# Five stages of a two-layer kernel written out sequence by sequence instead of in loops of two, with small moves in the first attention

## The reference, cut to what matters

```
x = layernorm(x + gated_state_space(x))       # layer 0, "attn": norm, 64-channel projection, norm,
                                              #   long convolution (kernel of 512 taps), gate, output
x = layernorm(x + latent_attention_and_moe(x))# layer 0, "ffn": rms norm, low-rank q/k/v with rotary parts,
                                              #   16 causal heads of 8; then a shared expert and 7 routed
                                              #   experts (top 2) of width 128
x = layernorm(x + attention(x))               # layer 1, "attn": 16 causal heads of 8, dense
x = layernorm(x + moe(x))                     # layer 1, "ffn": top 2 of 8 experts of width 512
```

## Time and profile before

| | us |
|---|---|
| median of 3 runs (lowest, highest) | 3305.35 (3304.07, 3309.35) |
| the profiled execution's own time | 3310.25 |
| its span, first to last instruction | 3308.5 |

### The profile page before, as it was taken

The page is one execution under the profiler, slowest core; times in us unless marked ns, Lnnn a source line. Parts: engine busy times, 40 slices in busy tenths (PEclk is TensorE's granted clock), DMA queues, the critical chain, the costliest instruction groups (busy, mean ns, idle before and its releaser), DMA issues. The chain is left out here.

```text
span 3308.5 us, 51694 instructions
## 1 busy us (share of the span) xinstructions
PE 2513.5 (76%) x15431; PEld 1777.0 (54%) x15431; DVE 2159.5 (65%) x8218; ACT 1411.2 (43%) x2540; POOL 1300.9 (39%) x2522
## 2 busy tenths in 40 slices
PE   1455873999999999488887599999999732688972
PEld 1323662656665656366666465666666431576751
DVE  5733764777777777388887477767777340467674
ACT  0001321665555566112121266666666411576851
POOL 3210012555455554223221255555555457222166
PEclk9997995999999999699999599999999755799986
DMA  2143002232232231211110222222212251476762
GB/s 30 30 143 115 22 10 37 34 47 41 29 46 39 31 46 28 90 48 48 61 34 4 41 38 33 32 40 40 34 26 40 64 204 58 148 226 214 252 187 72
DMA packets 198712, 228.44 MB, mean 69 GB/s; under 512 B 48621, under 2 KB 148814, under 8 KB 190478
## 3 DMA queue, kind: packets, MB, share of 16 engines
q1 hardware_dynamic: 188302, 207.69, 26.1%
q0 software_dynamic: 8192, 16.79, 1.6%
q10 hardware_dynamic: 2048, 2.10, 0.2%
HBM read 132.55 MB, written 58.10 MB: 58 GB/s over the span
## 5 line engine op out<-in xcount | busy, mean ns | idle before, releaser
L1422 PE MATMUL banks<-Kb,Qb 96*128 96x512 f32 (+3 forms) x2048 | 625.5, 353 | 75.8 <-issue 37.0
L1431 PE MATMUL banks<-Qb,Kb 98*128 98x512 f32 (+1 forms) x1408 | 580.0, 418 | 27.3 <-ACT mha_prob L1323 16.5
L1095 DVE CUSTOM_DVE_ANT_0 mha_junk<-banks,mha_mask 128x512 bf16<-128x512 f32 (+3 forms) x1024 | 455.5, 488 | 212.8 <-PE banks L1422 200.2
L1095 DVE CUSTOM_DVE_ANT_0 mla_junk<-banks,mla_mask 128x512 bf16<-128x512 f32 (+3 forms) x1024 | 455.3, 488 | 190.0 <-PE banks L1422 156.9
L1422 PEld LDWEIGHTS banks<-Kb,Qb 96*128 96x128 f32 x2048 | 377.1, 199 | 327.1 <-DVE mha_nm L1095 105.8
L1323 ACT ACTIVATE mla_prob<-banks 128x512 f32<-128x512 f32 (+1 forms) x704 | 372.9, 559 | 304.0 <-PE banks L1431 302.7
L1323 ACT ACTIVATE mha_prob<-banks 128x512 f32<-128x512 f32 (+1 forms) x704 | 373.5, 559 | 269.8 <-PE banks L1431 265.7
L1218 POOL TENSOR_SCALAR_AFFINE_SELECT mla_prob<-mla_prob 128x128 f32<-128x128 f32 (+2 forms) x704 | 237.8, 346 | 330.6 <-PEq L1430 323.4
L1218 POOL TENSOR_SCALAR_AFFINE_SELECT mha_prob<-mha_prob 128x128 f32<-128x128 f32 (+2 forms) x704 | 238.1, 347 | 301.0 <-PEq L1430 289.7
L1431 PEld LDWEIGHTS banks<-Qb,Kb 98*128 98x128 f32 x1408 | 273.3, 195 | 115.5 <-issue 97.9
L2198 DVE TENSOR_TENSOR moe_hl<-moe_h,moe_hh 128x512 fp32r<-128x512 f32 x212 | 146.1, 690 | 199.6 <-issue 95.1
(11 more groups left out here) (436 smaller groups left out, 5181.1 us busy)
## 6 DMA issues: line engine op xcount, KB each, us to landing
moe_wt<-expert_rows SPq DMA_DIRECT2D x53, 1024.0 KB
conv_tz<-conv_kernel SPq DMA_DIRECT2D x16, 1024.0 KB, 6.2
moe_xg<-slots SPq DMA_DIRECT2D x53, 256.0 KB
results<-moe_yt SPq DMA_DIRECT2D x53, 256.0 KB
Kb<-mla_kh SPq DMA_DIRECT2D x32, 256.0 KB, 5.5
Qb<-mla_qh SPq DMA_DIRECT2D x128, 64.0 KB
Kb<-mha_kh SPq DMA_DIRECT2D x32, 256.0 KB, 5.5
Qb<-mha_qh SPq DMA_DIRECT2D x128, 64.0 KB
```

Of the source, the lines that this page charges most:

```text
L1095: last = dve.tensor_tensor_reduce(junk[:, k % 3, at:at + w], ps[:, bank1(k), at:at + w], mask[:, L - w:L], -1.0, BIG, ALU.add, ALU.min, nm ...
L1422: last = pe.matmul(ps[:, bank1(k), at:at + w], Qb[0:MROW, u, g, h, j * P:(j + 1) * P], Kb[0:MROW, u, g, 0:w], start=True, stop=True)
L1431: pe.matmul(ps[:, bank2(g, k), 0:WIDE[k]].rearrange("p (x w) -> p x w", x=heads), Kb[0:MROW + 2, u, grp, kb * P:(kb + 1) * P], Qb[0:MROW + ...
```

## The change: what it does

In the walks of five stages (input, gate, both attentions, shared and routed experts) the loop over pairs becomes straight code, one copy for each sequence; `settle` goes from all of them, and semaphores count up through the stage. In the input stage the loops of ScalarE and TensorE go too. The loops of SyncE in the input, gate and experts stages, of GpSimd in the gate stage and all of the convolution stage stay. In the attentions' tables some places are moved: in the latent one the two key products, the statistics, `inverse_rms` and the two `prepare` steps; in both of them `NEXT`, by one unit.

```diff
@@ walk_sequences
     body(0, 0, False, True, True)
-    c.settle()
-    with eng.Fori(0, (NB - 2) // 2, 1) as i:
-        for v in range(2):
-            body(i * 2 + (v + 1), (v + 1) % 2, True, True, True)
-        c.settle()
+    for n in range(1, NB - 1):
+        body(n, n % 2, True, True, True)
     body(NB - 1, (NB - 1) % 2, True, True, False)
@@ input_stage, ScalarE (TensorE in the same way, its body unchanged)
-                with act.Fori(0, NB // 2, 1) as i:
-                    for u in range(2):
-                        act.wait_ge(t_ready, c.next(t_ready))
-                        act.activation(xth[:, u, :], ps[:, 1 + u, :], ACT.Copy).then_inc(th_ready, 1)
-                    c.settle()
+                for n in range(NB):
+                    u = n % 2
+                    act.wait_ge(t_ready, c.next(t_ready))
+                    act.activation(xth[:, u, :], ps[:, 1 + u, :], ACT.Copy).then_inc(th_ready, 1)
@@ attention_stage, tables
         if latent:
-            KEYS = dict(pe=((0, 10), (0, 11)), turn=(1, 1), add=(1, 2), act=(1, 5), low=(1, 7))
+            KEYS = dict(pe=((0, 11), (1, 0)), turn=(1, 1), add=(1, 2), act=(1, 5), low=(1, 7))
             QUERIES = dict(pe=((1, 6), (1, 8)), turn=(1, 10), add=(1, 11), act=(2, 3), low=(2, 5))
-            NEXT_XS = dict(stats=(2, 8), rms=(2, 11), scale=((3, 1), (3, 3)))
+            NEXT_XS = dict(stats=(2, 6), rms=(2, 9), scale=((3, 0), (3, 2)))
...
-        NEXT = dict(pe=(3, 6), act=(3, 7), dve=(3, 9))
+        NEXT = dict(pe=(3, 7), act=(3, 8), dve=(3, 10))
@@ attention_stage, walk
             body(0, 0, "first", True, True, False)
-            c.settle()
             body(1, 1, "inner", True, True, False)
-            c.settle()
-            with eng.Fori(0, (NB - 4) // 2, 1) as i:
-                for v in range(2):
-                    body(i * 2 + (v + 2), v, "inner", True, True, True)
-                c.settle()
+            for n in range(2, NB - 2):
+                body(n, n % 2, "inner", True, True, True)
@@ swiglu_experts_stage, walk
             tile(0, 0, True, 2)
-            c.settle()
-            with eng.Fori(0, (NB - 4) // 2, 1) as i:
-                for v in range(2):
-                    tile(i * 2 + (v + 1), (v + 1) % 2, False, 2)
-                c.settle()
-            for n in range(NB - 3, NB):
+            for n in range(1, NB):
                 tile(n, n % 2, False, min(2, NB - 1 - n))
```

More of the change, by code:

```diff
@@ L429, in _ @@
                 pe.sem_inc(d_free, 2)
[L430 to L444, removed]
-                    c.settle()
+                for n in range(NB):
+                    u = n % 2
+                    pe.wait_ge(xh_ready, c.next(xh_ready))
+                    for b in range(BLK):
+                        last = pe.transpose(ps[:, 1 + u, b * P:(b + 1) * P], xh[:, u, b, :], flip[:, :])
+                    last.then_inc(t_ready, 1)
+                    pe.wait_ge(t_split, c.next(t_split))
+                    pe.wait_ge(d_free, c.next(d_free))
+                    for b in range(BLK):
+                        o = ps[:, 3 + u, b * NC:(b + 1) * NC]
+                        tok = slice(b * P, (b + 1) * P)
+                        pe.matmul(o, xth[:, u, tok], wdh[:, :], start=True, stop=False)
+                        pe.matmul(o, xth[:, u, tok], wdl[:, :], start=False, stop=False)
+                        last = pe.matmul(o, xtl[:, u, tok], wdh[:, :], start=False, stop=True)
+                    last.then_inc(d_ready, 1)
 def convolution_stage(nc, io, ps, U, kd, yd):
```

## The result

| | us |
|---|---|
| kernel before, same chip and session, median of 4 | 3307.35 (3304.07 to 3312.17) |
| changed kernel, median of 4 (lowest, highest) | 3219.80 (3218.61, 3221.26) |
| ratio, 95% interval | 0.9734 [0.9717, 0.9751] |
| the changed kernel's profiled execution, its span | 3219.59, 3217.8 |

The account below looks back on a forecast made before the run. TensorE's order was taken to bound the attentions, VectorE's the experts, with time lost at loop seams. Gains 29.9 + 24.9 + 8.1 + 0 + 9.2 + 1 = 73.1 us, from 3305.35 to 3232; 8 in 10 range 3214 to 3256.

Parts of the forecast that it names:

- The likeliest case: Whole kernel: straight code runs every turn like turn 2, with no jump; 3232 us, own range 3224 to 3242, 62%.
- first attention, loop: Turns 2 to 13 of the first attention each take turn 2's 46.70 us: gain 28.8 us.
- second attention, loop: Turns 2 to 13 of the second attention each take turn 2's 44.36 us: gain 23.8 us.
- the slower rival: Straight code throughout: fetched code comes late and stops TensorE at all 67 fetches, 105 us lost, 3337 us; 5%.
- The clock: Attentions: TensorE's clock falls after standing twice near a seam, 2.98 us in one turn; straight turns run at 1.00.
- the clock stays: Rival, attentions: pauses go, but TensorE still falls to 1.2 GHz as often; 21 us not gained, 3253 us; 13%.
- The moves: Attention tables: moved places gain 1 us in the first attention (bounds -7 and 8.5), 0 in the second.
- The stall of "about 0.5": First attention, unit (2, 10): moved statistics delay VectorE, so TensorE waits for a bank, about 0.5 us a turn.
- Input: Input stage: VectorE's wait at the seam goes in 7 passes, gain 8.1 us (bounds 0 and 10).
- Experts: Layer 0 experts: six seams at 1.42 us and half a seam after tile 0, gain 9.2 us.
- Second attention: Second attention: 23.8 us from the loop and 1.1 for two settles, gain 24.9 us (bounds 0 and 27).
- Gate: Gate stage: VectorE's pause is covered by its own wait, gain 0; bounds a gain of 6 or loss of 19.

Follow-up runs that it names:

- run 5: Changed kernel with VectorE alone looping in all five walks, all other engines straight: 3150.69 us, beside 3152.05 of the kernel before.
- run 10: Changed kernel plus six tiny two-round loops of one semaphore increment on VectorE alone in each attention: 3082.75 us.
- run 9: Changed kernel with a hardware loop of two passes of six sequences put back in the walks: 3118.33 us, against 3080.20 of the changed kernel.
- run 2: Changed kernel with the moved places undone, straight code alone: 3079.55 us, ratio to the kernel before 0.9721.
- run 12: The changed kernel itself, measured again on another chip beside the best version: median 3080.20 us, ratio to the kernel before 0.9734.
- run 1: Kernel before with its loops kept, only the moved places in the attention tables: 3152.15 us against 3163.40, ratio 0.9976.
- run 3: Changed kernel, straight, but with the subtractions of `settle` kept wherever a pass ended: 3106.28 us.
- run 4: Changed kernel with only VectorE straight in all five walks, the other engines looping as before: 3101.28 us, beside 3152.05 of the kernel before.
- Run 11: Changed kernel, first attention's query copy one unit earlier, statistics and `inverse_rms` moved back, VectorE alone looping over pairs in the gate: 3066.35 us, ratio to before 0.9699.

## Why the prediction was right, and where its sizes were off

The likeliest case held, and its reason; the total fell below its range, and 7.0 us of the miss lie in a last stage that the change doesn't touch. The two large terms were read from turn 2, and nearly every turn became one: *first attention, loop* 28.7 measured for 28.8, *second attention, loop* 25.2 for 23.8. Turns 0 and 1 gave 2.0 and 2.3 instead of 1.1 each; in the first attention turn 14 is 1.1 longer than before, so its stage is 28.3 where 29.9 + 1 stood.

The inference on which this rested, "VectorE has to fetch its code again after it has jumped back", is borne out from four sides: only VectorE's loop brings the pause (run 5), a jump to a tiny body doesn't (run 10), in the experts stage VectorE gets it only when its body is made longer (run 9), and TensorE gets a pause of the same kind with longer bodies too (run 9). In the input stage, where VectorE's body is short (95 instructions), its jump never had one: the 1.30 of the earlier trace rows are seven subtractions at 0.09 and the jump itself. What no row shows is the wait for a named fetch; the queues' counts and places agree with it. One reading of the prediction was wrong: it priced a late fetch by TensorE's 1.57 at the seam, but that was subtractions and a branch. The pause that goes with TensorE's fetches is the 4.3 to 4.6 of run 9. The Trainium skill, Advanced Engine Details and Errata, section ISA Cache, gives TensorE four times the store of the others, and the order in which the two engines begin to pause agrees: counting every row of a pass, VectorE jumps back over 221 instructions without a pause and over 362 with one, TensorE over 1355 without and over 1554 with one, so the ratio of the two lengths lies between 3.7 (1355 to 362) and 7.0 (1554 to 221). The sizes themselves no run here shows.

- *The clock* was put down to seams, rightly for the attentions: clock 1.00 in both, falls gone. The rival "the clock stays" is out there.
- *The moves* (+1): right for this kernel, -1.2 in the turns (runs 2 and 12: 559.31, 558.34 and 560.47 differ by about what one profile differs from the next). The stall of "about 0.5" came as 0.45. "A TensorE that comes sooner waits as much longer" is a small part of it, 0.2 a turn at the boundary; the larger part the prediction called hidden, the key products, which put into group 1 the 0.7 that they take out of group 0. In the looped kernel the turns were 7 us shorter (run 1), which I had not expected; that TensorE's shorter turn spares it clock there is a guess.
- *Input* (8.1, measured 13.3): the seam's 8.1 are near right (six seams of 1.15 and a last one, not jumped, of 0.7), the step that is missing is register arithmetic. In a loop each address that depends on the counter is computed by the engine that uses it: up to ten instructions of 53 to 117 ns on VectorE a turn, 0.37 us that no row of idle time names. 14 x 0.37 = 5.2. The sign "input turns at 7.9" was wrong with it: they take 7.50.
- *Experts* (9.2, measured 12.7): tile 7, my yardstick, itself carried 0.13 of the loop, so twelve tiles give 6 x 1.55 + 6 x 0.13 = 10.1 instead of 8.5; another 2.1 is the first seam, where the clock fell in the kernel before (tiles of 28.63 and 26.44). Of the 1.7 that two looped tiles cost over two straight ones the subtractions are 0.95 (run 3); the rest is the jump and the registers.
- *Second attention* (24.9, measured 29.4 for the stage, 27.6 from its first to its last reduction): 1.4 more in turns 2 to 13, 1.2 more before them, and 1.8 at the stage's edges, which is less than what two profiles of one kernel differ by there. That the 1.4 are the registers no run isolates.
- *Gate* (0, measured -0.8; the turns alone -2.1): a clean turn is 0.13 shorter, 11.20 for 11.33, but the clock falls in every second turn, seven times for four. The bound of a loss was there, its size was small.
- *Not in the sum*: 7.0 us in the last stage and 0.8 in the convolution, whose code didn't change. Across chips the last stage varies by 150 us, so this is no effect of the change that the runs show.

By these the sum, 73.1, missed 5.2 + 3.5 + 4.5 - 2.6 - 0.8 + 0.8 + 7.0 = 17.6 of 90.7. The last two terms are no effect of the change that a run shows: without them the time would be some 3227. The turns say more for the prediction than the total does. The fetches of fresh straight code, the slower rival's ground, cost nothing that can be seen.

Open: why the gate's clock falls in a fixed rhythm, 23.9 us apart, six or seven times, in every run where VectorE is straight there (run 4 too, where the others loop) and in run 9, and less often (2 to 4 times) wherever VectorE loops over pairs. Run 11 uses it; nothing explains it.

## What to carry to other kernels

In a loop whose turns do equal work compare the first turn of the first pass with the mean of all: the difference times the turns is what straight code gives back, and in the attentions it held to 0.1 and 1.4 us. It misses what the first turn carries too: in the input stage turn 1 of the loop has the registers like the others. A seam on the engine with the largest body that doesn't stay in its store is worth more than all others: look for a few us of idle time on it right after the jump with its input ready, then ask what runs dry behind it, and whether the clock falls. Longer bodies with fewer jumps are a poor bargain: two passes of six have one jump a stage instead of six or seven, and kept 45 us of the gain of 84, since a longer body brings the pause to stages and engines that had none.

## What was not expected of the hardware

- A jump back costs VectorE some tenths of a us after a short body; after one of two attention turns (some 316 busy instructions) its next instruction comes 2.8 us behind the branch, after six expert tiles as well. TensorE's branch takes 0.2 us after 614 matmuls, 4.58 after some 1840.
- Subtracting from a semaphore takes 0.09 us on VectorE and 0.15 on TensorE for each. Ten of them before VectorE's first instruction of an expert tile make 0.95 us of a seam.
- Register arithmetic for addresses is paid by the busy engine at 53 to 117 ns each and shows in no line of idle time of the page.
- A pause of one engine can cost more on another: behind VectorE's pause, 3.4 us longer than a straight boundary (4.6 against 1.2 from reduction to reduction), TensorE's clock fell to 1.2 GHz, for another 2 us (turns of 48.8 against 46.7) in the first attention. Not every pause does it: the first seam of the second attention has VectorE's 3.83 us and no fall.
